# Fewer, larger DMA transfers around the scan of a two-layer kernel: four transfers for each batch become one, and the intermediate x1 is kept in tiles

## What is computed

```python
xr, gate = split(x @ W_in.T); xc = silu(causal_conv(xr + t_emb) + b_conv)
xn = layernorm(xc) * ln_g + ln_b                       # 4 x 1024 x 1024
Bm, Cm, dt = split(xn @ W_xproj.T)                      # 16 states each
# scan over the 1024 positions, h is 16 x 1024 for each batch
h = clip(h * Ad + Bd * xn[t], -10, 10);  y[t] = Cm[t] . h
x1 = x + ((y + D * xn) * silu(gate)) @ W_out.T          # residual of layer 1
# layer 2 on x1: scale by the style, layernorm, q, k, v, attention (16 heads), w, skip through u
out = x1 + attention_layer(x1)
```

## Time and profile before

| | |
|---|---|
| median of 3 runs | 2892.28 us (2890.06 to 2894.39) |
| the profiled execution | 2890.06 us |
| its span | 2888.3 us |
| instructions | 55551 |
| PE, DVE, ACT, POOL busy | 93%, 69%, 41%, 44% of the span |
| granted TensorE clock, mean | 0.962 of full speed |
| moved by DMA | 424.01 MB, mean 147 GB/s |

### The profile page before, as it was taken

How to read it: one execution, slowest core, us unless ns; L and a number is a source line. 1 busy time by engine, 2 the same in 40 slices (tenths; PEclk the granted TensorE clock), 3 DMA queues, 4 the chain that set the end, 5 groups by cost and what they waited for, 6 DMA issues and landing times. The chain is left out here.

```text
span 2888.3 us, 55551 instructions
## 1 busy us (share of the span) xinstructions
PE 2680.0 (93%) x20490; PEld 1461.4 (51%) x20490; DVE 2000.3 (69%) x2112; ACT 1189.9 (41%) x2039; POOL 1280.6 (44%) x583
## 2 busy tenths in 40 slices
PE   7999954999999999999979999969999999999999
PEld 3444332666666666666657877833333333333337
DVE  2789866888888888888843333367677677677726
ACT  2677851222222122222232122126666666666641
POOL 0000001555555555555541212026667777777763
PEclk9999966999999999999989999979999999999999
DMA  3246575877777778777744344472244344344247
GB/s 106 88 153 222 181 242 138 162 173 159 167 173 163 168 166 169 166 160 176 147 144 171 128 145 156 148 196 65 69 110 111 89 128 109 94 125 118 81 175 227
DMA packets 260284, 424.01 MB, mean 147 GB/s; under 512 B 59368, under 2 KB 127592, under 8 KB 253752
## 3 DMA queue, kind: packets, MB, share of 16 engines
q1 hardware_dynamic: 177848, 332.86, 42.7%
q10 hardware_dynamic: 82304, 89.44, 12.5%
HBM read 260.91 MB, written 163.08 MB: 147 GB/s over the span
## 5 line engine op out<-in xcount | busy, mean ns | idle before, releaser
L917 DVE CUSTOM_DVE_ANT_0 b_h<-b_h,b_bx,b_bounds_all 128x512 f32<-128x512 f32 x1024 | 825.7, 806 | 157.2 <-PE b_bx L1062 108.3
L1617 DVE TENSOR_REDUCE e_half_max<-ef_banks 128x4 f32<-128x2048 f32 x256 | 586.2, 2293 | 234.6 <-PE ef_banks L1570 234.6
L1760 POOL TENSOR_TENSOR e_pair_sum<-e_probs 128x2048 f32<-128x2048 f32 x128 | 586.7, 4584 | 265.2 <-PE ef_banks L1609 214.1
L1729 ACT ACTIVATE e_probs<-ef_banks 128x512 f32<-128x512 f32 x1024 | 556.0, 595 | 310.9 <-PE ef_banks L1584 310.8
L1584 PE MATMUL ef_banks<-e_qs,e_ks 97*128 97x512 f32 x1024 | 382.5, 453 | 3.9 <-DVE e_half_max L1617 3.6
L1118 ACT COPY d_v_rows<-b_y_psum 128x128 f32<-128x128 f32 x256 | 68.2, 266 | 682.6 <-PE b_y_psum L1072 682.6
L1584 PEld LDWEIGHTS ef_banks<-e_qs,e_ks 97*128 97x128 f32 x1024 | 154.8, 189 | 331.9 <-ACT e_probs L1729 311.7
L1062 PE MATMUL b_bx<-b_x_moving,b_b_weights 24*128 24x512 f32 x1024 | 257.9, 499 | 67.1 <-DMA b_x_moving<-xn_parts 37.0
L1042 POOL TENSOR_TENSOR b_b_weights<-b_bd,b_mask_b 128x512 fp32r<-128x512 f32 x64 | 82.5, 1288 | 520.8 <-POOLq L841 459.1
L1072 PE MATMUL b_y_psum<-b_h,b_c_weights 128*32 128x128 f32 x8224 | 279.8, 277 | 11.4 <-ACT d_v_rows L1118 11.4
L1594 PE MATMUL ef_banks<-e_probs,e_v 128*32 128x512 f32 x2048 | 274.4, 608 | 0.5 <-ACT e_probs L1729 0.4
(11 more groups left out here) (226 smaller groups left out, 4052.4 us busy)
## 6 DMA issues: line engine op xcount, KB each, us to landing
b_x_moving<-xn_parts SPq DMA_DIRECT2D x252, 128.0 KB
e_ks<-qk_parts ACTq DMA_DIRECT2D x42, 512.0 KB, 4.8
e_qs<-qk_parts ACTq DMA_DIRECT2D x84, 256.0 KB, 3.5
xn_full<-a_xn SPq DMA_DIRECT2D x32, 512.0 KB, 3.2
xn_parts<-a_hi SPq DMA_DIRECT2D x64, 256.0 KB, 2.5
xn_parts<-a_lo SPq DMA_DIRECT2D x64, 256.0 KB, 2.5
silu_gate<-d_v_rows ACTq DMA_DIRECT2D x64, 256.0 KB, 6.3
shared<-xn_full SPq DMA_DIRECT2D x128, 128.0 KB, 6.3
```

Of the source, the lines that this page charges most:

```text
L917: return nc.vector._custom_dve(bass.dve_ops.TENSOR_ADD_SAT, **operands)
L1617: nc.vector.tensor_reduce(out=half_max[:, u // UNITS % 2, :, r // NH, r % NH], in_=(banks[:, u % 2 * GROUP:(u % 2 + 1) * GROUP] if u < FIR ...
L1729: nc.scalar.activation(probs[:, g % 4, h, :], p_exp[h % 2], ACT.Exp).then_inc(exps, 1)
L1760: nc.gpsimd.tensor_tensor(out=pair_sum[:, t % 2], in0=probs[:, (2 * t) % 4], in1=probs[:, (2 * t + 1) % 4], op=ALU.add).then_inc(paired, 1)
```

## The change

- `load_mixed` loads xn of a tile with one transfer and not four of 32 rows each; `load_y` does the same with y.
- The scratch tensor `X1` is laid out as 32 tiles of 128 rows (`x1_tiles`: 32 positions of four batches, as the tile lies in SBUF) and not as batch x position. `store_x1` stores a tile with one contiguous transfer and not four.
- `load_x1` therefore reads its 128 positions of one batch from four tiles, 32 rows in each; it is one transfer as before.
- `x` is handed over in its plain layout (4 x 1024 x 512) and not tiled by the host; `load_x` reads 32 rows of each of the four batches in one transfer.
- The counts of the semaphore waits follow: 32 and not 80 for xn and silu(gate), 16 and not 64 for y and x1.

```diff
     def load_x1(self, sp, n, q):
-        sp.dma_start(self.x1[:, q, :], self.X1[bass.ds(n, 1)].rearrange("o (q t) c -> (o q) t c", q=NQ)[q]).then_inc(self.x_in[q], 16)
+        sp.dma_start(self.x1[:, q, :], self.X1.rearrange("(q i) (b t) c -> b q i t c", q=NQ, b=BATCH)[bass.ds(n, 1)].rearrange("o q i t c -> (o q) i t c")[q]).then_inc(self.x_in[q], 16)
...
         def load_mixed(sp, j):
             sp.wait_ge(gated, START + j)
-            for b in range(BATCH):
-                sp.dma_start(xn[b * STEPS:(b + 1) * STEPS, :], Xn[b, bass.ds(j * STEPS, STEPS), :]).then_inc(xn_in, 16)
+            sp.dma_start(xn, Xn[:, bass.ds(j * STEPS, STEPS), :]).then_inc(xn_in, 16)
...
         def load_y(sp, j):
...
-            for b in range(BATCH):
-                sp.dma_start(y[b * STEPS:(b + 1) * STEPS, :], Y[bass.ds(j * STEPS, STEPS)].rearrange("t (h b) c -> b t h c", h=2)[b]).then_inc(y_in, 16)
+            sp.dma_start(y[:], Y[bass.ds(j * STEPS, STEPS)].rearrange("t (h b) c -> b t h c", h=2)).then_inc(y_in, 16)
         def load_x(sp, j):
             sp.wait_ge(x1_ready, START + j)
-            sp.dma_start(x[:], I["x"][bass.ds(j, 1)].rearrange("o p c -> (o p) c")).then_inc(res_in, 16)
+            sp.dma_start(x[:], I["x"][:, bass.ds(j * STEPS, STEPS), :]).then_inc(res_in, 16)
         def store_x1(sp, j):
             sp.wait_ge(x1_ready, START + j + 1)
-            for b in range(BATCH):
-                sp.dma_start(X1[b, bass.ds(j * STEPS, STEPS), :], x1[b * STEPS:(b + 1) * STEPS, :]).then_inc(x1_out, 16)
+            sp.dma_start(X1[bass.ds(j, 1)].rearrange("o p c -> (o p) c"), x1[:]).then_inc(x1_out, 16)
...
-            e.wait_ge(xn_in, START + j * 80 + 80)
+            e.wait_ge(xn_in, START + j * 32 + 32)
...
-            e.wait_ge(y_in, START + j * 64 + 64)
+            e.wait_ge(y_in, START + j * 16 + 16)
...
-    X1 = scratch("x1_full", [BATCH, SEQ, MODEL])
+    X1 = scratch("x1_tiles", [NQ * BATCH, P, MODEL])
```

More of the change, by code:

```diff
@@ L931, in add_x @@
             e.wait_ge(res_in, START + j * 16 + 16)
-            e.wait_ge(x1_out, START + j * 64)
+            e.wait_ge(x1_out, START + j * 16)
             engine.tensor_tensor(out=x1[:], in0=x[:], in1=o[:], op=ALU.add).then_inc(x1_ready, 1)
@@ L1192, in _ @@
                 load_mixed(sp, last)
-                sp.wait_ge(x1_out, START + (last - 3) * 64)
+                sp.wait_ge(x1_out, START + (last - 3) * 16)
                 for q in early_tiles[:3]:
@@ L1208, in _ @@
                 store_x1(sp, last)
-                sp.wait_ge(x1_out, START + TILES * 64)
+                sp.wait_ge(x1_out, START + TILES * 16)
                 pj.load_x1(sp, 0, NQ - 1)
@@ L1310, in body @@
                                 sp.dma_start(dst, t[:, e % 2, :].bitcast(f32)).then_inc(qk_out[e % 2], 16)
-                sp.wait_ge(pj.x1_out, START + BATCH * NQ * 64)
+                sp.wait_ge(pj.x1_out, START + BATCH * NQ * 16)
                 batches(sp, body)
@@ L1424, in body @@
                             dve.wait_ge(rows_in, START + 16 + 16 * BATCH)
-                            dve.wait_ge(pj.x1_out, START + BATCH * NQ * 64)
+                            dve.wait_ge(pj.x1_out, START + BATCH * NQ * 16)
                         if 0 <= q < NQ:
@@ L1938 @@
     arrays = {
-        "x": np.ascontiguousarray(np.asarray(inputs["x"]).reshape(BATCH, SEQ * BATCH // P, P // BATCH, MODEL).transpose(1, 0, 2, 3)).reshape(SEQ * BATCH // P, P, MODEL), "x_t": np.ascontiguousarray(np.asarray(inputs["x"]).transpose(0, 2, 1)), "x_tiles": np.ascontiguousarray(np.asarray(inputs["x"]).reshape(BATCH, SEQ * BATCH // P, P // BATCH, NK, P).transpose(1, 4, 3, 0, 2)).reshape(SEQ * BATCH // P, P, NK, P),
+        "x": plain("x"), "x_t": np.ascontiguousarray(np.asarray(inputs["x"]).transpose(0, 2, 1)), "x_tiles": np.ascontiguousarray(np.asarray(inputs["x"]).reshape(BATCH, SEQ * BATCH // P, P // BATCH, NK, P).transpose(1, 4, 3, 0, 2)).reshape(SEQ * BATCH // P, P, NK, P),
         "t_emb": plain("cond_2048"),
```

## The result

The changed kernel takes 3116.8 us (median of 4 runs, 3114.3 to 3127.13), the kernel before in the same session 2891.17 us: a ratio of 1.0789, 95% interval 1.076 to 1.0819. The forecast of 2926 us had the sign right and the size wrong by 191 us, and the time lies outside the range. The profiled execution has a span of 3120.0 us, 231.7 us more than before.

A forecast was written before the change was run, and what follows sets the result against it. SP's issue queue in front of x_moving was taken to pace the scan loop; +23 us loop and +13 us hand-over made +36 us on 2890.1, so 2926 us. Forecast's own range 2900 to 2965, overall range 2830 to 2995.

The forecast's parts named there:

- What bounds the kernel now: Scan loop: SP's issue queue delays x_moving; 30.2 us an iteration against 27.3 without waits, at most 84 us to gain.
- What the change takes away: SP's queue in the loop: nine of 33 issues an iteration go, so x_moving is issued 3.5 us earlier.
- Narrow transfers: Loads of xn, y, x and load_x1: with 4 outermost, done by four of 16 DMA engines, 25 GB/s each.
- the sources are not narrowed: Rival for the merged loads: engines shared out by the target's 128 rows; 2804 us, chance 0.07.
- they stay hidden: Rival at each iteration's end: narrow loads stay hidden, earlier x_moving wins; 28.5 us an iteration, 2854 us, chance 0.27.
- The load on those four engines: Scan loop: 22.5 us by bytes plus 8 for bursts, 31.0 with gaps against 30.2 now; +23 us.
- The extra of the bursts: Two x_moving bursts an iteration hold the engines 10 us beyond their bytes; 8 us charged to the four engines.
- check of the DMA share: Scan loop: 0.42 for bytes plus 0.33 for the bursts' extra makes 0.75; the trace shows 0.77.
- Half a microsecond of gaps: Four engines' queue in the loop: y waits for scan_out to land, adding half a microsecond, making 31.0 us.
- The hand-over: From scan to projections: y's end 9 us later, four other load_x1 add 4; +13 us, bounds +9 and +17.
- The projections at zero: 24 more load_x1 land about 2 us later, covered by over 7 us; zero, without cover 6 us.
- saturated: Rival in the loop: bursts at full price, SP behind full queues; 33.5 us an iteration, about 2999 us, chance 0.18.

The follow-up runs named there:

- e4: Kernel before with only x1 kept in tiles: one contiguous store, load_x1 as one narrow load from four tiles; 2845.94 us, ratio 0.9852.
- e6: Kernel before with x1 in tiles, stored in one contiguous transfer, but load_x1 as four loads of 32 rows; 2843.55 us, ratio 0.9826.
- e7: Kernel before with the store of x1 and load of x issued behind the eight first-half loads of x_moving; 2837.07 us, ratio 0.9805.
- e13: Kernel before with the x_moving loads bringing half from the fourth iteration on, for timing alone; 2834.84 us, ratio 0.9801.
- e5: Kernel before with only x in plain layout, still one load, its source 4 batches of 32 rows; 2999.7 us, ratio 1.0365.
- e9: e6 with x in plain layout, loaded by four loads of 32 rows each; 2859.79 us, ratio 0.9881.
- e10: Kernel before with only x in plain layout, in two loads of two batches each; 3083.81 us, ratio 1.0662.
- e11: e5 with the store of x1 and load of x issued behind the first eight x_moving loads, as in e7; 2938.7 us, ratio 1.0156.
- e14: Changed kernel with the x_moving loads bringing half from the fourth iteration on, for timing alone; 2988.81 us, ratio 1.0339.
- e8: Changed kernel with the store of x1 and load of x issued behind the eight first-half loads of x_moving; 3148.45 us, ratio 1.088.
- e1: Kernel before with its four loads each of xn and y kept, HBM side written as 4 groups of 8 rows; 2889.17 us, ratio 1.0000.

## Why the prediction was wrong

- **What bounds the kernel now: right.** e4, e6, e7 and e13 each take work or issues from in front of `x_moving` and all end at 28.4 or 28.5 us an iteration, with at most 2.2 us of wait for it in 700. Only the floor was off: I took 27.3 us from 16 steps in a row, but an iteration has short gaps at its start, and the runs show 28.4. The most to be had in the loop was 29 x 1.8 = 52 us, not 84.
- **What the change takes away: right.** 3.4 us less between the issues of y and `x_moving`, as counted. e4 turns its share of them into 44 us; in the changed kernel no gain is seen.
- **Narrow transfers: right.** Four engines for 4 outermost (e5 against e9), and two for 2 (e10). The rival that the sources are not narrowed is out, and so is the one that they stay hidden.
- **The load on those four engines: this step failed.** It put a loop of 31.0 us against a measured 37.3, and its upper bound (32.5 us and one of gaps) lies below that too. The term that was mis-sized is the price of a narrow transfer beside a burst. I priced its bytes at the 25 GB/s of an engine in a calm stretch and charged the bursts a fixed extra of 8 of their 10 us. What the runs show is that the two work on each other: x alone, 2.0 us by bytes, costs 3.6 us an iteration against before and 5.4 against a free loop (e5), also with its place in the queue changed (e11), and with the bursts halved the loss of the whole change in the loop falls from 9.3 to 3.7 us (e14).
- **The extra of the bursts was put in the wrong place.** Between 600 and 1300 of before, the 8 KB packets of `x_moving`, 192 in an iteration, take 0.69 us each in the mean, where 25 GB/s would make 0.33: 4.4 us an iteration for each of sixteen engines, not 10. The rest of the extra is with the packets beside them: SP's 2 KB packets take 0.13 us in the mean for 0.08, its 4 KB packets 0.28 for 0.16. Those are the packets that the change puts on four engines. The prediction's check of the DMA share (0.75 against 0.77) could not tell the two apart. The eight-row loads of `x_moving`, whose 1.3 us the prediction left out of its sum, seem to belong in it: exactly eight packets are in flight for 3.3 us of before's iteration, longer than any other number from 1 to 14.
- **Half a microsecond of gaps: too little.** I treated the four engines as a queue that is always full. But y waits for scan_out, `x_moving` is issued behind y, and POOL's weights stand behind the mix with y: each late transfer makes the next one start late. e8, e11 and e14 show the wait at this last link, where `x_moving` is on time or nearly so. The packets in flight, those of 256 bytes and more, counted over 600 to 1300, bound both terms (us of an iteration):

| kernel | iteration | fewer than 4 | 4 to 6 | 7 or more |
|---|---|---|---|---|
| before | 30.2 | 2.9 | 1.3 | 26.0 |
| after | 37.7 | 3.3 | 12.2 | 22.2 |
| e13 | 28.4 | 9.2 | 2.5 | 16.7 |
| e14 | 32.1 | 6.4 | 12.3 | 13.4 |

While fewer than four are in flight, not all of the four engines can be at work. So in after they stand partly idle for at least 3.3 us where I had 0.5, and all four are at work for at most 34.4 us, where I had 30.5. In e14 the work is the 25.5 us that the same account gives, at most 25.7, and the iteration is 6.4 us longer: this points to the waits from one transfer to the next, and not the load, as what sets the time there.

- **How the parts add up.** Against before, the single parts (+3.1 us an iteration for xn, +2.9 for y, +3.6 for x, -1.7 for x1) sum to +7.9, and all together make +7.5. This is no proof that they act independently: against the free loop of 28.4 us, xn, y and x cost 4.9, 4.7 and 5.4 us, 15.0 in sum, and together 9.3.
- **A term that was missing: TensorE's clock.** While PE waits 15 us, the granted clock in the windows goes from 1.00 to 0.50, the lower of its levels (1.2 of 2.4 GHz), and the first products behind the wait take 0.79 us for 0.50. Timelines of DVE behind the wait, after and then before:

```profile
928.28 3.33 DVE L914 CUSTOM_DVE_ANT_0 b_h<-b_h,b_bx,b_bounds_all 128x512 f32<-128x512 f32 x4 [2.68 <-PE b_bx L1059]
```

```profile
932.47 6.79 DVE L917 CUSTOM_DVE_ANT_0 b_h<-b_h,b_bx,b_bounds_all 128x512 f32<-128x512 f32 x8 [0.77 <-PE b_bx L1062]
```

  The second wait of DVE is 2.68 us at the low clock and 0.77 behind a wait of 2.43 us at the full one. As the long wait (11 to 15 us) comes in every second iteration, an estimate from these two rows is (2.68 - 0.77)/2, about 1 us an iteration of the 7.
- **The hand-over: right in kind, low in size.** The add with y is 12.7 us later where I had 9; the whole is 17.3 where I had 13, with bounds of 9 and 17. The term that was low is the wait for the queue ahead of y, in which SP itself is stopped: y is issued 4.7 us later and takes 8.0 us longer from there to the add. The 4 us for the other four `load_x1` came out as counted (16.7 - 12.7).
- **The start: missing.** The first three iterations already suffer, by 15.8 us, and I had counted them at zero.
- **The projections at zero: right.** From the last `load_x1` on, the two kernels differ by 0.6 us, and e4 and e6 cannot be told apart.
- Of the rivals, *saturated* (2999 us) had the nearest mechanism, and it too was 118 us short. Its sign, long issues of SP in the loop, did not show: y's issue takes 0.58 us in the iteration shown; where SP was seen held up is the hand-over.
- The upper end of the forecast's own range does not follow from its working: 32 us an iteration and 13 us of hand-over make 2955 us, and not 2965. The measured time is far outside either.

Open is how the 7 us of an iteration divide exactly. The packets bound the idle time and the work of the four engines, but the trace does not say on which engine a packet ran, and no run keeps the loads narrow while it takes the dependences between them away.

## What to carry to other kernels

Before four DMAs are merged into one, look at the outermost dimension of both sides: one issue of 4 outermost frees three issues of SP (0.7 us each for y) and moves all its bytes over a quarter of the engines. Merge where the HBM side becomes one contiguous block (the store of x1: faster by 44 us), and leave rows in separate loads where it doesn't. Don't price such a transfer by its bytes and a calm stretch's rate: look for the bursts that run at the same time, and for who waits next. If the issue queue is the bound, moving the uncritical issues behind the critical ones (e7, 60 us) got all that merging could in this loop.

## What the hardware showed that was not expected

- All 16 engines can be busy (share 1.03 to 1.06) and move only 137 to 142 GB/s, when the narrow load of x and the burst of `x_moving` are on the way together (e5); a calm mix reached 398. Beside the burst a packet of 2 KB takes 0.30 us in the median (893 to 896 of e5), in the calm mix 0.084.
- The cost of the narrow load of x did not depend on its place in the queue: +103 us ahead of the burst (e5), +102 behind it (e11, over e7).
- Writing contiguous rows as four groups of 8 changed neither landing nor time nor the number of packets in flight (e1).
